# Cross-attention with layernorm: the high part of q laid twice over the rows, two of three score products merged, and the start of the kernel reordered

## The reference

```python
qs  = (q @ wq).reshape(Bq, Lq, H, HD).transpose(0, 2, 1, 3)      # q = x, 4 x 2048 x 512
ks_ = (k @ wk)...                                                # k = v = ctx, 4 x 77 x 512
vs  = (v @ wv)...
scores = einsum('bhqd,bhkd->bhqk', qs, ks_) / sqrt(HD)
scores = where(mask, -inf, scores)
attn = softmax(scores) @ vs                                      # then heads side by side
out = attn @ wo + q
return (out - mu) / sqrt(var + EPS) * gamma + beta
```

## Time and profile before

| | |
|---|---|
| time of the profiled execution | 635.87 us |
| its span (first to last instruction) | 633.7 us |
| median of the runs | 635.59 us |
| PE busy | 613.4 us, 97% |
| DVE, ACT, POOL busy | 83%, 80%, 78% |
| granted TensorE clock, mean | 0.999 |

### The profile page before, as it was taken

How to read it: one execution, slowest core, us unless ns; L and a number is a source line. 1 busy time by engine, 2 the same in 40 slices (tenths; PEclk the granted TensorE clock), 3 DMA queues, 4 the chain that set the end, 5 groups by cost and what they waited for, 6 DMA issues and landing times.

```text
span 633.7 us, 12457 instructions
## 1 busy us (share of the span) xinstructions
PE 613.4 (97%) x3820; PEld 485.0 (77%) x3820; DVE 527.3 (83%) x1007; ACT 509.0 (80%) x1558; POOL 494.6 (78%) x639
## 2 busy tenths in 40 slices
PE   7998999999999999999999999999999999999995
PEld 5766687887878788787878878787887878787763
DVE  4867797987889788888889988887898988789887
ACT  3877888888888888888987988898888888787851
POOL 5476568797978979796987979698897879677785
PEclk9999999999999999999999999999999999999999
DMA  8450213221231323123241312223122222502103
GB/s 282 153 190 16 76 34 105 80 100 51 101 111 68 103 80 102 55 95 100 71 134 57 101 59 92 100 86 112 55 101 66 84 85 67 167 34 67 52 34 117
DMA packets 34785, 57.75 MB, mean 91 GB/s; under 512 B 6816, under 2 KB 7840, under 8 KB 34720
## 3 DMA queue, kind: packets, MB, share of 16 engines
q1 hardware_dynamic: 34720, 56.96, 27.0%
HBM read 39.53 MB, written 16.78 MB: 89 GB/s over the span
## 4 chain that ended last, share of the span: by engine, by line
PE 79%; DVE 10%; ACT 3%; POOL 3%; issue 2%; DMA 1%; SPq 1%; POOLq 0%; DVEq 0%
PE bank L311 23%; PE bank L393 23%; PE bank L334 15%; PE bank L344 8%; PE bank L365 4%; PE bank L370 2%; PE bank L348 2%; ACT pr L498 2%; DVE pr L635 2%; DVE sm L648 1%; DVE nm L641 1%; DMA ptr<-xT 1%; PE bank L304 1%; DVE kl L606 1%; DVE ql L623 1%
## 5 line engine op out<-in xcount | busy, mean ns | idle before, releaser
L498 ACT ACTIVATE pr<-pr,nm 128x77 f32<-128x77 f32 x1024 | 270.1, 348 | 64.7 <-DVE nm L641 62.7
L799 POOL TENSOR_TENSOR pn<-pr,rec 128x512 f32<-128x512 f32 x128 | 135.0, 1055 | 91.6 <-DVE rec L650 89.9
L635 DVE SCALAR_TENSOR_TENSOR pr<-msk,bank 128x308 f32<-128x308 uint8 x256 | 109.4, 469 | 39.7 <-PE bank L334 38.4
L648 DVE TENSOR_REDUCE sm<-pr 128x8 f32<-128x616 f32 x128 | 99.8, 780 | 12.0 <-ACT pr L498 10.6
L641 DVE TENSOR_REDUCE nm<-pr 128x8 f32<-128x616 f32 x128 | 101.8, 795 | 4.4
L311 PE MATMUL bank<-xh,wqh 128*128 128x512 f32 x256 | 103.0, 402 | 1.3 <-DVE ql L623 1.3
L467 ACT ACTIVATE ptr<-bank 128x512 f32<-128x512 f32 (+1 forms) x256 | 95.5, 426 | 9.7 <-PE bank L344 9.6
L393 PE MATMUL bank<-woh,ah 128*128 128x512 f32 x256 | 101.7, 397 | 1.4 <-DVE al L657 1.4
L393 PE MATMUL bank<-woh,al 128*128 128x512 f32 x256 | 101.2, 395 | 0.0
L393 PE MATMUL bank<-wol,ah 128*128 128x512 f32 x256 | 101.1, 395 | 0.0
L311 PE MATMUL bank<-xh,wql 128*128 128x512 f32 x256 | 100.7, 393 | 0.0
(11 more groups left out here) (69 smaller groups left out, 1060.2 us busy)
## 6 DMA issues: line engine op xcount, KB each, us to landing
xraw<-xT SPq DMA_DIRECT2D x59, 256.0 KB, 3.0
xres<-x SPq DMA_DIRECT2D x58, 256.0 KB, 2.7
out<-y SPq DMA_DIRECT2D x56, 256.0 KB, 2.1
wk_sb<-wk SPq DMA_DIRECT2D x4, 256.0 KB, 4.4
wq_raw<-wq SPq DMA_DIRECT2D x4, 256.0 KB, 6.7
wv_sb<-wv SPq DMA_DIRECT2D x1, 1024.0 KB, 9.3
wo_raw<-xT SPq DMA_DIRECT2D x4, 256.0 KB, 9.3
wo_raw<-wo SPq DMA_DIRECT2D x1, 1024.0 KB, 5.4
```

The costliest lines, as they stand in the source:

```text
L498: last = nc.scalar.activation(s, s, ACT.Exp, bias=nm[:, t % 2, h:h + 1], scale=1.0)
L635: nc.vector.scalar_tensor_tensor(out=pr[:, 4 * g:4 * g + 4, :], in0=msk[:, b % 2, t % TB, :].unsqueeze(1).broadcast_to([P, 4, LK]), scalar ...
L648: nc.vector.tensor_reduce(sm[:, t % 2, hs], pr[:, hs, :], AX.X, ALU.add).then_inc(v_sum, 1)
L799: nc.gpsimd.tensor_tensor(pn[:, half, 0:4, :].rearrange("p s (e k) -> p (s e) k", e=2), pr[:, hs, 0:KM], rec[:, t % 2, hs].unsqueeze(2).br ...
```

## The change

Two copies of the high part of q stand in one tile `qd`: for each piece m and half u, rows 64u to 64u + 63 of q fill rows 0 to 63 and again rows 64 to 127. Opposite to them `kd` holds the high part of the keys in rows 0 to 63 and the low part in rows 64 to 127, two heads (154 columns, `PW`) at a time. One matmul of 154 columns then sums high by high and high by low for two heads. A group of scores is a matmul of 308 columns (ql by kh) and two of 154, from block 1 on. In block 0, whose q high part stands in `ah` instead, a group is four matmuls: 308, 154, 308 and 154 columns.

`qd` is filled by DMAs from `qn` (`double_q`, four per piece, 64 rows of 2 KB each), 16 per block, in tiles with t % 4 == 3; `kd` by `pair_k` (12 DMAs, once) and DVE. `kt`, the low parts in rows as they are made, lies in the place of `qd` and is set to zero by POOL before DVE writes it. Further: in tiles with t % 4 == 3 the q projection and the output projection change places; the first two score groups of tile 0 stand before the q projection of piece 3; V is projected before tile 0, in tile 1, and half each in tiles 3 and 4, and placed in tiles 0, 2 and 5; wo comes in four pieces through `gam` and `bet`, which are loaded in tile 7; `split_wo` stands ahead of `normalise`.

```diff
-                    for n, (w, s) in enumerate(((qh, kh), (qh, kl), (ql, kh))):
-                        last = nc.tensor.matmul(o, w[blk % 2][:, g, r * P:(r + 1) * P], s[:, g, t // TB, :],
-                                                start=(n == 0), stop=(n == 2))
+                    nc.tensor.matmul(o[:, 0:GW], ql[blk % 2][:, g, r * P:(r + 1) * P], kh[:, g, t // TB, :],
+                                     start=True, stop=False)
+                    if blk == 0:
+                        nc.tensor.matmul(o[:, 0:PW], qk[0][:, g, r * P:(r + 1) * P], kt[:, g, t // TB, :], ...)
+                        nc.tensor.matmul(o[:, 0:GW], qk[0][:, g, r * P:(r + 1) * P], kh[:, g, t // TB, :], ...)
+                        nc.tensor.matmul(o[:, PW:GW], qk[0][64:128, g, r * P:(r + 1) * P], kd[64:128, g, 1, t // TB, :], ...)
+                        continue
+                    if r == 0:
+                        pe.wait_ge(d_qd[g], 64 * blk)
+                        if blk == 1:
+                            pe.wait_ge(d_kd[g], 48)
+                    for u in range(2):
+                        last = nc.tensor.matmul(o[:, u * PW:(u + 1) * PW], qd[:, g, u, r * P:(r + 1) * P],
+                                                kd[:, g, u, t // TB, :], start=False, stop=(u == 1))
...
+            def double_q(i):
+                blk, m = i // 4, i % 4
+                sp.wait_ge(p_s, NG * (4 * blk - 1) + m + 1)
+                if i == 4:
+                    for g in range(NG):
+                        sp.wait_ge(d_kd[g], 48)
+                sp.wait_ge(a_qh, i + 1)
+                for u in range(2):
+                    for v in range(2):
+                        sp.dma_start(qd[64 * v:64 * v + 64, m, u].bitcast(f32), qn[64 * u:64 * u + 64, m].bitcast(f32)
+                                     ).then_inc(d_qd[m], 16)
...
             for t in range(T + LAG):
+                if t % 4 == 3 and t < T - 4:
+                    double_q(t + 1)
+                    double_q(t + 2)
                 if t >= 1 and t + 10 < 4 * NBLK:
                     load_slice(t + 10)
...
-                if 1 <= t <= 3:
-                    sp.wait_ge(a_v, t)
-                    for b in ((0,), (1, 2), (3,))[t - 1]:
+                if t in PLACE:
+                    sp.wait_ge(a_v, PLACE[t] + 1)
+                    for b in ((0,), (1, 2), (3,))[PLACE[t]]:
                         place_v(b)
...
                     sp.dma_start(out_v[o], y_of(o)).then_inc(d_y[o % YS], 16)
+                if t % 4 == 3 and t < T - 4:
+                    double_q(t + 3)
+                    double_q(t + 4)
...
-            dve.wait_ge(g_z, 1)
+            dve.wait_ge(g_z, 2)
...
+            for n in range(4):
+                low_x(n)
+            pool.wait_ge(v_w, KT)
+            pool.wait_ge(p_k, NG)
+            nc.gpsimd.memset(kt.bitcast(f32), 0.0).then_inc(g_z, 1)
```

More of the change, by code:

```diff
@@ L12 @@
 GW = 4 * LK
+PW = 2 * LK
 NG = 4
@@ L34 @@
 LAG = 6
+V_AT = {1: (1,), 3: (2, range(0, 2)), 4: (2, range(2, 4))}
+V_KEPT = {2: 1, 5: 2}
+PLACE = {0: 0, 2: 1, 5: 2}
 LAST = T - 8
@@ L129, in z_of, with wo_of @@
         def z_of(o):
-            return z[:, o % 2] if o < VFIN else wv_sb[:, o - VFIN] if o < VFIN + KT else xraw[:, o - VFIN - KT]
+            return z[:, o % 2] if o < VFIN else zt[:, o - VFIN if o < VFIN + KT else o - VFIN + KT]
+        def wo_of(k):
+            return (gam, bet)[k % 2]
         def y_of(o):
@@ L140, in cross_attention_layernorm @@
         d_wq = [sem(f"d_wq{k}") for k in range(KT)]
-        d_wv, d_wo = (sem(n) for n in ("d_wv", "d_wo"))
+        d_wo = [sem(f"d_wo{k}") for k in range(KT)]
+        d_wv = sem("d_wv")
         d_vm = [sem(f"d_vm{i}") for i in range(2)]
@@ L147, in cross_attention_layernorm @@
         d_y = [sem(f"d_y{i}") for i in range(YS)]
+        d_kd = [sem(f"d_kd{g}") for g in range(NG)]
+        d_qd = [sem(f"d_qd{g}") for g in range(NG)]
         d_end, d_xe = sem("d_end"), sem("d_xe")
@@ L269, in _ @@
                     sp.dma_start(out_v[o], y_of(o)).then_inc(d_y[o % YS], 16)
+                if t % 4 == 3 and t < T - 4:
+                    double_q(t + 3)
+                    double_q(t + 4)
+                if t in (1, 2):
+                    sp.wait_ge(g_wo, 2 * t)
+                    sp.dma_start(wo_of(t + 1)[:], w_v(wo)[:, t + 1, :]).then_inc(d_wo[t + 1], 16)
+                if t == 7:
+                    sp.wait_ge(g_wo, 2 * KT)
+                    sp.dma_start(gam[:], gamma.partition_broadcast(P)).then_inc(d_gb, 16)
+                    sp.dma_start(bet[:], beta.partition_broadcast(P)).then_inc(d_gb, 16)
+                if t == 5:
+                    sp.wait_ge(d_vm[1], 32 * 16)
+                    for o in range(XR):
+                        load_res(o)
                 if 0 <= t - LAG < VFIN - XR:
@@ L294, in _, with project_v @@
                         mm.then_inc(p_k, 1)
-            def project_v(i):
+            def project_v(i, ks=range(KT)):
                 if i == 0:
                     pe.wait_ge(d_wv, 16)
-                if i < 2:
-                    pe.wait_ge(v_ql, i + 3)
-                else:
-                    pe.wait_ge(a_v, 1)
-                for k in range(KT):
+                if ks[0] == 0:
+                    if i < 2:
+                        pe.wait_ge(v_ql, i + 3)
+                    else:
+                        pe.wait_ge(a_v, 1)
+                for k in ks:
                     last = nc.tensor.matmul(AVB[i % 2][0:VC[i + 1] - VC[i], :], ctx_sb[:, k, VC[i]:VC[i + 1]], wv_sb[:, k, :],
                                             start=(k == 0), stop=(k == KT - 1))
-                last.then_inc(p_v, 1)
+                if ks[-1] == KT - 1:
+                    last.then_inc(p_v, 1)
             def project_q_slice(i, k):
@@ L545, in _ @@
             keep_x(5)
+            keep_x(6)
+            exps(0, 0)
             keep_q(3)
-            for n in range(6, 8):
-                keep_x(n)
+            keep_x(7)
+            keep_v(0)
             for t in range(T - 4):
-                if t >= 1:
+                if t in V_KEPT:
+                    keep_v(V_KEPT[t])
+                if t % 4 > 0:
                     keep_q(t + 3)
@@ L557, in _ @@
                     standardise(t - LAG - 1)
-                exps(t, 0)
-                if t == 0:
+                if t >= 1:
+                    exps(t, 0)
+                else:
                     keep_x(8)
-                if t < 3:
-                    keep_v(t)
                 if t in VALUES:
@@ L606, in low_k @@
                     nc.vector.scalar_tensor_tensor(
-                        out=kl[rows, g, :, j * LK:(j + 1) * LK],
+                        out=(kd[rows, g, 1] if j >= 2 else kt[rows, g])[:, :, j % 2 * LK:(j % 2 + 1) * LK],
                         in0=bank[g][rows, 0:NB * LK].rearrange("p (b k) -> p b k", b=NB), scalar=SCALE,
@@ L709, in _ @@
                     low_q(t + 3)
-                mask_max(t, 0)
-                if t >= 1 and t not in VALUES:
+                if t >= 1:
+                    mask_max(t, 0)
+                if t % 4 > 0 and t not in VALUES:
                     low_q(t + 3)
@@ L717, in _ @@
                 mask_max(t, 1)
+                if t % 4 == 3:
+                    low_q(t + 4)
                 row_sums(t, 0)
@@ L727, in _ @@
             mask_max(T - 4, 0)
-            low_q(T - 1)
             mask_max(T - 4, 1)
```

110 lines of the change are left out of this document (69 added, 41 removed).

## The result

The changed kernel takes **671.23 us** (median of 6 runs, 666.75 to 674.30) against 636.88 for the kernel before beside it (635.58 to 639.71): ratio 1.053, 95% interval 1.049 to 1.058. It is 5.3% slower. Forecast were 635, range 617 to 650. The profiled execution took 671.11 us, with a span of 668.9 instead of 633.7, so 35.2 us have to be found.

What follows compares the result with a forecast made beforehand. PE was taken to bound the kernel, busy 478.35 of 480 us in the middle. Profiled 635.9 + 12 (start) + 1 (steady copies) - 13.5 (score groups) = 635.4, forecast 635 us, range 617 to 650.

Steps and rivals of the forecast that it cites:

- The new score group: PE's score groups from block 1 on: 0.36 us instead of 0.42 each, gain 13.5 us in all.
- both rival values: 154-column matmul on PE: 0.07 us (loads hide better, to 617 us, chance 0.17) or 0.14 (no gain, 649, 0.05).
- The start: Tiles before tile 6: late copies into `qd` delay PE, loss 12 us, bounds 4 and 17.
- (a): First tiles: `low_k` also waits for POOL's zeroing of `kt` and starts 3.3 us later, at 20.4.
- (b, c): V's placement by SP: second third kept at 45.7 instead of 41.1, then 18.9 us of issues, ending at 64.6.
- (d): First 16 copies into `qd`, behind V's placement: 0.47 us an issue, last one lands at 74.7.
- (e): Last group of tile 4: PE waits until 74.7, ends 10.1 us late; tile 5 starts 12 us later than 67.84.
- The steady copies: Later blocks: 16 more SP issues, 7.5 us per block, nearly all in time; 1 us for all blocks.
- deciding point: Copy issue on SP: above 0.5 us each, group 3 of each block's first tile waits.
- Copies late in every block: Rival: SP issues of 0.74 us cost 18 in 15 blocks and 4.6 more in the start, 658 us; chance 0.13.
- What else moves: Other engines and queues: `gam` and `bet` late in tile 8, POOL's some 3 us wait absorbed; no new bound.
- Sum: Whole kernel: 635.9 + 12 + 1 - 13.5 = 635.4 us, two large terms cancelling.

Runs made afterwards that it cites:

- copies_once: The changed kernel with copies into `qd` made for block 1 only, later blocks multiplying those rows again; 646.03 us, ratio 1.016.
- gam_tile6: The changed kernel with gamma and beta loaded in SP's tile 6 instead of tile 7; 663.9 us, ratio 1.044.
- v_split: The changed kernel with V of batch 2 placed behind the first 16 copies into `qd`, not ahead of them; 666.07 us, ratio 1.046.
- the two edits further ahead: Two separate edits of the changed kernel: fourth q projection ahead of the first scores, 666.9 us; zeroing of `kt` in four pieces, 665.86 us.
- copies_half_bytes: The changed kernel with each copy moving 256 of the 512 queries from the second copied block on; 663.62 us, ratio 1.043.
- the orders: The changed kernel with copies, output and load of x reordered on SyncE's queue at a block's end, three ways; 676.74, 666.34 and 662.41 us.
- the two queues: The changed kernel with copies to the upper row half issued by ScalarE instead of SyncE; 664.7 us alone, 660.12 us with all other edits.

## Why the prediction was wrong, step by step

**The new score group: right.** Forecast 0.36 us, measured 0.36 to 0.37; with 0.07 or 0.14 for a 154-column matmul it would be 0.28 or 0.42, so both rival values are out. The Trainium skill (TensorE: Matmul & The Clock Gate, "Back-to-back issue gap") spoke for 81 ns a pair of load and matmul at 128 columns; here the loads of these matmuls start 0.11 us apart, and the measurement decides against it. The sum was 13.0 us over tiles 6 to 59 and came out as 9.8 (`copies_once`): tiles that multiply by V gained 0.12, not 0.24, and tiles 19, 20, 35, 36, 51 and 52 nothing. In 19, 35 and 51 the wait for DVE's `ql` took it (0.43 us before, 0.74 in `copies_once`). The rest is open.

**The start: the chain was right, its sizes were not.** Forecast +12, measured +20.4 at tile 6. (a) `low_k` started 2.9 us later, as forecast (3.3), but I let its effect end there. PE idled 2.4 us at 24.8, went to the lower clock and was 6.6 us late at tile 1. (b, c) V was placed from 48.71, not from 45.7, for 18.6 us (18.9 forecast); in `gam_tile6`, where the clock stayed up, it was placed from 45.73, so the sum had the waits and lacked the clock. (d) The 16 copies took 9.97 us for 0.62 each, not 7.5. The last landed at 80.9 instead of 74.7. (e) Behind the waits the clock was 0.50 from 75 to 85 us: tile 5 began at 88.5, not at 80. `v_split` took 10.4 us off the start of tile 6, so V's placement ahead of the copies was the right link. For the two edits further ahead a gain of under 1 us stands beside the same start with the clock up.

**The steady copies: the step that failed.** "I put 1 us for all blocks." The openings came out 17.2 us longer. The forecast took the issue of a plain load, 0.47 with its gap, for a copy between partitions. It is 0.62, above my own deciding point of 0.5. The rival "Copies late in every block", with 0.13, was what happened. Its price of 18 for the blocks is near the 17.2 measured by luck: it took 0.74 an issue, and 2.6 of the 17.2 (tile 12) went away with the wait for beta. Its 4.6 in the start was too low. `copies_half_bytes`, the orders and the two queues show that both parts count: issues at 0.62 in a row and the landing at 2.4.

**What else moves.** "POOL waits some 3 us; its 17% of free time takes that" was wrong. The wait was 4.71, and it was on the chain: tile 9 lost 4.4, and `gam_tile6` gave tiles 9 and 12 7.1 back. Free time as a share says nothing about one late item when DVE, ACT and then PE take their input from it within the tile. Here I had again used the plain issue time: `bet` stands behind 16 copies.

**Sum.** 12 + 1 - 13.5 was forecast; 20.4 + 4.4 + 17.2 - 7.3 = 34.7 was found at tile 60 (34.6 by its starts). Of some 35 us of error, 16 lie in the steady copies, 8 in the start (3 of them the lower clock at 25 us), 4 in beta and 6 in the gain (the openings' share of it is inside their 17.2).

## What to carry to other kernels

A copy that must wait until its target is read has a budget: the time from the last read to the next. Write down the issues in that row, with a price from rows of the same kind of copy, add the landing, and compare; here 10.7 + 2.4 = 13.1 stood against 12.3. A second target buffer might take the row off the path; it was not tried. A wait on PE can cost nearly double, for the clock behind it, and this changes from one execution to the next. So before an edit at the start gets the credit, compare it with other executions of the same start.
